# Mixture rows turned by DMA transposes instead of TensorE, two groups ahead

## The reference, cut to what matters

```python
# h: (64, 197, 192); every token is a row of 192 numbers
x2 = layernorm(h).reshape(-1, 192)
weights, indices = gate(x2, gate_weight, gate_bias)   # sigmoid scores, 2 of 4 groups, 2 of 8 experts
h1 = einsum('td,eid->tei', x2, w1)                    # eight experts, each 192 -> 128
h3 = einsum('td,eid->tei', x2, w3)
y  = einsum('tei,edi,te->td', silu(h1) * h3, w2, cw)  # weighted by the gate
z  = silu(x2 @ sw1.T) * (x2 @ sw3.T) @ sw2.T          # a shared expert, added without a weight
out = h + y + z
```

## Time and profile before

| what | value |
|---|---|
| median of three runs | 1811.99 us |
| profiled execution, its own time | 1810.96 us |
| its span | 1809.2 us |
| second stage, from the first load of `hin` | from 1048.72 us to the end |
| PE / DVE / ACT / POOL busy over the span | 94% / 72% / 54% / 19% |

### The profile page before, as it was taken

One profiled execution on the slowest core, in us unless ns is written; L12 is line 12 of the kernel. 1 busy time (PEld: TensorE's weight loads), 2 busy tenths in 40 slices (PEclk: granted clock), 3 DMA queues, 4 the chain that ended last, 5 costly groups with the idle time before them and its releaser, 6 DMA issues. The chain is left out here.

```text
span 1809.2 us, 45442 instructions
## 1 busy us (share of the span) xinstructions
PE 1704.5 (94%) x17682; PEld 1172.8 (65%) x17682; DVE 1297.7 (72%) x3626; ACT 978.8 (54%) x2079; POOL 336.6 (19%) x402
## 2 busy tenths in 40 slices
PE   1899999999999999999999859999999999999998
PEld 1677777777777777777777535555565555555555
DVE  4566666666666666666666448888888888888887
ACT  2466656656655655566666534545545454545453
POOL 1000000000000000000000014343434444343433
PEclk9999999999999999999999969999999999999999
DMA  6232333322223332233330010101010000001000
GB/s 203 62 72 72 73 72 73 72 66 68 69 71 73 72 70 69 72 72 73 72 72 19 15 39 19 36 18 36 19 37 27 28 28 27 28 27 35 17 18 16
DMA packets 40866, 95.26 MB, mean 53 GB/s; under 512 B 4491, under 2 KB 17454, under 8 KB 40526
## 3 DMA queue, kind: packets, MB, share of 16 engines
q1 hardware_dynamic: 31438, 72.89, 12.9%
q0 software_dynamic: 9216, 19.47, 7.0%
HBM read 92.44 MB, written 19.37 MB: 62 GB/s over the span
## 5 line engine op out<-in xcount | busy, mean ns | idle before, releaser
L598 ACT ACTIVATE prob<-ps_sc 99x792 f32<-99x792 f32 x384 | 317.3, 827 | 56.4 <-PE ps_sc L440 56.4
L1259 POOL TENSOR_TENSOR in_lo<-inner,in_hi 128x512 f16<-128x512 f32 (+1 forms) x225 | 257.6, 1145 | 433.6 <-ACT act L1046 433.2
L1192 DVE SCALAR_TENSOR_TENSOR acc<-ps_y,comb,acc 128x192 f32<-128x192 f32 (+1 forms) x700 | 242.0, 408 | 0.3 <-PE ps_y L988 0.3
L1054 ACT ACTIVATE in_hi<-inner 128x512 f16<-128x512 f32 (+1 forms) x225 | 140.3, 623 | 181.3 <-DVE inner L1174 181.3
L1046 ACT ACTIVATE act<-ps_h 128x512 f32<-128x512 f32 (+1 forms) x225 | 131.7, 585 | 189.7 <-PE ps_h L972 189.7
L1174 DVE SCALAR_TENSOR_TENSOR inner<-ps_h,act 128x512 f32<-128x512 f32 (+1 forms) x225 | 153.8, 683 | 103.3 <-ACT act L1046 99.6
L383 PE MATMUL ps_hid<-lin_hi,x_hi 128*99 128x192 f16 x768 | 191.0, 249 | 39.0 <-DVE x_lo L661 34.9
L986 PE MATMUL ps_y<-w_hi,in_hi 128*128 128x192 f16 (+1 forms) x900 | 223.9, 249 | 4.0 <-DVE acc L1192 2.6
L987 PE MATMUL ps_y<-w_lo,in_hi 128*128 128x192 f16 (+1 forms) x900 | 221.4, 246 | 0.0
L988 PE MATMUL ps_y<-w_hi,in_lo 128*128 128x192 f16 (+1 forms) x900 | 221.4, 246 | 0.0
L807 POOL DMA_DIRECT2D x_hi<-xp x64 | 34.0, 532 | 915.4 <-PE ps_hid L385 893.7
(11 more groups left out here) (156 smaller groups left out, 3658.6 us busy)
## 6 DMA issues: line engine op xcount, KB each, us to landing
xin<-xp SPq DMA_DIRECT2D x64, 594.0 KB, 4.4
x_hi<-xp POOLq DMA_DIRECT2D x64, 297.0 KB, 4.0
hidden_dram<-h SPq DMA_DIRECT2D x64, 147.0 KB
hin<-hidden_dram SPq DMA_DIRECT2D x24, 384.0 KB, 3.0
out<-acc SPq DMA_DIRECT2D x24, 384.0 KB, 2.3
w_f<-w SPq DMA_DIRECT2D x1, 2304.0 KB, 9.9
hidden_dram<-h SPq DMA_DIRECT2D x64, 0.8 KB
w_f<-w SPq DMA_DIRECT2D x1, 864.0 KB, 11.9
```

The source lines that it names most:

```text
L598: act.activation(prob[quad][:, places].rearrange("p h m s -> p h (m s)"), ps_sc[0:TR, places, 0:2 * SLOTS], ACT.Exp, scale=D ** -0.5 / (SQ ...
L1192: last = dve.scalar_tensor_tensor(out=acc[p][0:R, t, :], in0=ps_y[half_no][0:R, u * C:(u + 1) * C], scalar=comb[p][0:R, t, e:e + 1], in1=b ...
L1259: pool.tensor_tensor(in_lo[b][:, 0:N], inner[b][:, 0:N], in_hi[b][:, 0:N], ALU.subtract).then_inc(inlo_done, 1)
```

## The change

The normalised rows are no longer turned by TensorE. ScalarE normalises two groups ahead (steps 5 and 6) and writes the fp16 high part `y_hi` from `bnorm` by rows; VectorE writes the low part `y_lo` (steps 6 and 7); SyncE then issues 16-bit DMA transposes of `y_hi` and `y_lo` into `yT_hi` and `yT_lo`, now rings of three. That is four lanes of two transposes, eight for each group, each of 128 rows by 256 columns (columns 192 to 255 repeat 128 to 191). The factor 64 (`SX`) moves from the copies into `rstds`. `y_hi` and `y_lo` have one buffer each, so ScalarE waits with the next group's `y_hi` until the transposes before have landed (`yT_in`). The statistics are at steps 2 and 3, `rstds` moves from behind step 5 to behind step 4, the gate's matmuls from step 4 to step 3, its `Tanh` (`gate_out`) from step 4 to 3, and the parts of `route` from steps 5 to 8 to steps 4, 5, 6 and 8. TensorE's gate waits for all eight transposes. The two banks `ps_x` become one, `ps_gate`.

```diff
@@ -829,9 +829,11 @@
-        bnorm = sb("bnorm", [128, T, 256])
-        yT_hi = [sb(f"yT_hi{p}", [128, 2, GT], F16) for p in range(2)]
-        yT_lo = [sb(f"yT_lo{p}", [128, 2, GT], F16) for p in range(2)]
+        bnorm = sb("bnorm", [128, T, C])
+        y_hi = sb("y_hi", [128, T, 256], F16)
+        y_lo = sb("y_lo", [128, T, 256], F16)
+        yT_hi = [sb(f"yT_hi{p}", [128, 2, GT], F16) for p in range(3)]
+        yT_lo = [sb(f"yT_lo{p}", [128, 2, GT], F16) for p in range(3)]
...
@@ -912,12 +915,29 @@
                 sp.wait_ge(acc_done, g.times(2 * NE, 2 * NE))
                 sp.dma_start(part(tokens_out, g), acc[p][0:rows_of(g)]).then_inc(acc_out[p], 16)
 
+            def transposes(g, half_no):
+                R, p = rows_of(g), g.mod(3)
+                sp.wait_ge(ylo_done, g.times(2, half_no + 1))
+                if half_no == 0 and reached(g.times(NE, -2 * NE)):
+                    sp.wait_ge(inner_done, g.times(NE, -2 * NE))
+                for t in (2 * half_no, 2 * half_no + 1):
+                    s = slice(t * R, (t + 1) * R)
+                    sp.dma_start_transpose(yT_hi[p][:, :, s], y_hi[0:R, t, :]).then_inc(yT_in[p], 16)
+                    sp.dma_start_transpose(yT_lo[p][:, :, s], y_lo[0:R, t, :]).then_inc(yT_in[p], 16)
+
             for g in range(3):
                 load(Index(0, g, 2, GROUPS_B))
+            for g in range(2):
+                transposes(Index(0, g, 2, GROUPS_B), 0)
+                transposes(Index(0, g, 2, GROUPS_B), 1)
 
             def body(g):
+                ahead = g.back(-2)
                 if g.back(-3).active():
                     load(g.back(-3))
+                if ahead.active():
+                    transposes(ahead, 0)
+                    transposes(ahead, 1)
                 store(g)
             run(body)
             sp.wait_ge(acc_out[0], 16 * (FULL // 2 + 1))
...
@@ -925,25 +945,15 @@
 
         @block.tensor
         def _(pe):
-            def transposes(g):
-                R = rows_of(g)
-                pe.wait_ge(bnorm_done, g.times(2, 2))
+            def gate(g):
+                R, p = rows_of(g), g.mod(3)
+                pe.wait_ge(yT_in[p], 32 * T * (g.c // 3 + 1))
 
                 if reached(g.times(1)):
                     pe.wait_ge(tanh_done, g.times(1))
                 for t in range(T):
                     s = slice(t * R, (t + 1) * R)
-                    for k in range(2):
-                        last = pe.transpose(ps_x[k][:, s], bnorm[0:R, t, k * 128:(k + 1) * 128], id32[0:R, 0:R])
-                last.then_inc(yT_done, 1)
-
-            def gate(g):
-                R, p = rows_of(g), g.mod(2)
-                pe.wait_ge(yThi_done, g.times(2, 2))
-                pe.wait_ge(yTlo_done, g.times(2, 2))
-                for t in range(T):
-                    s = slice(t * R, (t + 1) * R)
-                    dst = ps_x[0][0:R, t * E:(t + 1) * E]
+                    dst = ps_gate[0:R, t * E:(t + 1) * E]
                     pe.matmul(dst, yT_hi[p][:, 0, s], gate_hi[:, 0], start=True, stop=False)
                     pe.matmul(dst, yT_hi[p][:, 0, s], gate_lo[:, 0], start=False, stop=False)
                     pe.matmul(dst, yT_lo[p][:, 0, s], gate_hi[:, 0], start=False, stop=False)
...
@@ -1000,9 +1005,7 @@
                         outer_products(g, e - 2)
                     elif g.back(1).active():
                         outer_products(g.back(1), e + NE - 2)
-                    if e == 2 and following.active():
-                        transposes(following)
-                    if e == 4 and following.active():
+                    if e == 3 and following.active():
                         gate(following)
                 if not following.active():
                     outer_products(g, NE - 2)
...
@@ -1014,27 +1017,27 @@
             def normalise(g, half_no):
 
                 R, p = rows_of(g), g.mod(3)
+                ts = slice(2 * half_no, 2 * half_no + 2)
                 act.wait_ge(bneg_done, g.times(1, 1))
+                if reached(g.times(2, half_no - 1)):
+                    act.wait_ge(ylo_done, g.times(2, half_no - 1))
+                for t in (2 * half_no, 2 * half_no + 1):
+                    last = act.activation(bnorm[0:R, t, :], hin[p][0:R, t, :], ACT.Identity,
+                                          scale=brstd[0:R, t:t + 1], bias=bshift[0:R, t:t + 1])
+                last.then_inc(bnorm_done, 1)
+                act.wait_ge(bnorm_done, g.times(2, half_no + 1))
+
                 if half_no == 0 and reached(g.times(1)):
-                    act.wait_ge(yT_done, g.times(1))
-                for t in (2 * half_no, 2 * half_no + 1):
-                    for dst, src in ((slice(0, C), slice(0, C)), (slice(C, 256), slice(128, C))):
-                        last = act.activation(bnorm[0:R, t, dst], hin[p][0:R, t, src], ACT.Identity,
-                                              scale=brstd[0:R, t:t + 1], bias=bshift[0:R, t:t + 1])
-                last.then_inc(bnorm_done, 1)
-
-            def yT_out(g):
-                N, p = T * rows_of(g), g.mod(2)
-                act.wait_ge(yT_done, g.times(1, 1))
-                for k in range(2):
-                    act.activation(yT_hi[p][:, k, 0:N], ps_x[k][:, 0:N], ACT.Copy,
-                                   scale=SX).then_inc(yThi_done, 1)
+                    before = g.back(1)
+                    act.wait_ge(yT_in[before.mod(3)], 32 * T * (before.c // 3 + 1))
+                act.activation(y_hi[0:R, ts, 0:C], bnorm[0:R, ts, :], ACT.Copy)
+                act.activation(y_hi[0:R, ts, C:256], bnorm[0:R, ts, 128:C], ACT.Copy).then_inc(yhi_done, 1)
 
             def gate_out(g):
                 R = rows_of(g)
                 act.wait_ge(gate_done, g.times(1, 1))
 
-                act.activation(half[0:R], ps_x[0][0:R, 0:T * E].rearrange("p (t e) -> p t e", e=E), ACT.Tanh,
+                act.activation(half[0:R], ps_gate[0:R, 0:T * E].rearrange("p (t e) -> p t e", e=E), ACT.Tanh,
                                scale=0.5 / SS).then_inc(tanh_done, 1)
 
             def silu(g, e):
...
@@ -1054,21 +1057,21 @@
                 act.activation(in_hi[b][:, 0:N], inner[b][:, 0:N], ACT.Copy).then_inc(inhi_done, 1)
 
             first = Index(0, 0, 2, GROUPS_B)
+            second = first.back(-1)
             normalise(first, 0)
             normalise(first, 1)
-            yT_out(first)
+            normalise(second, 0)
+            normalise(second, 1)
             gate_out(first)
 
             def body(g):
-                following = g.back(-1)
+                following, ahead = g.back(-1), g.back(-2)
                 for e in range(NE):
                     silu(g, e)
                     inner_first(g, e)
-                    if e in (0, 1) and following.active():
-                        normalise(following, e)
-                    if e == 2 and following.active():
-                        yT_out(following)
-                    if e == 4 and following.active():
+                    if e in (5, 6) and ahead.active():
+                        normalise(ahead, e - 5)
+                    if e == 3 and following.active():
                         gate_out(following)
             run(body)
 
...
@@ -1088,13 +1091,13 @@
                 for t in ts:
                     dve.bn_aggr(bmv[0:R, t, :], bstats[0:R, t, :]).then_inc(bmv_done, 1)
 
-            def yT_out(g):
-                N, p = T * rows_of(g), g.mod(2)
-                for k in range(2):
-                    dve.wait_ge(yThi_done, g.times(2, k + 1))
-                    dve.scalar_tensor_tensor(out=yT_lo[p][:, k, 0:N], in0=ps_x[k][:, 0:N], scalar=SX,
-                                             in1=yT_hi[p][:, k, 0:N], op0=ALU.mult,
-                                             op1=ALU.subtract).then_inc(yTlo_done, 1)
+            def rest_of(g, half_no):
+                R = rows_of(g)
+                ts = slice(2 * half_no, 2 * half_no + 2)
+                dve.wait_ge(yhi_done, g.times(2, half_no + 1))
+                dve.tensor_tensor(y_lo[0:R, ts, 0:C], bnorm[0:R, ts, :], y_hi[0:R, ts, 0:C], ALU.subtract)
+                dve.tensor_tensor(y_lo[0:R, ts, C:256], bnorm[0:R, ts, 128:C], y_hi[0:R, ts, C:256],
+                                  ALU.subtract).then_inc(ylo_done, 1)
 
             ROUTE_STEPS = 19
             ROUTE_PARTS = (0, 3, 7, 11, 13, 15, ROUTE_STEPS)
...
@@ -1207,7 +1210,10 @@
             dve.wait_ge(bneg_done, 1)
             for half_no in range(2):
                 stats_of(second, half_no)
-            yT_out(first)
+            for half_no in range(2):
+                rest_of(first, half_no)
+            for half_no in range(2):
+                rest_of(second, half_no)
             for part_no in range(4):
                 route(first, part_no)
 
...
@@ -1221,12 +1227,14 @@
                         accumulate(g.back(1), e + NE - 2)
                     if e < 2:
                         route(g, e + 4)
```

(33 more changed lines are left out.)

## The result

The changed kernel takes 1879.2 us (median of four runs, 1877.71 to 1879.72) against 1812.47 before: a ratio of 1.037, with a 95% interval of 1.0352 to 1.0388. It is slower by 67 us, where 42 were forecast (1854). That is as forecast in sign and in the wait that starts the loss. The time lies above the forecast's own range (1840 to 1872) and inside the range over all (1836 to 1970), which was stretched upwards for slow transposes.

The account below looks back on a forecast made before the run. TensorE's own instruction list was taken as the bound. Stalls of 23 x 2.6 = 59.8 us less 20.9 saved, +38.9, and +3.5 at the start gave 1854 us; own range 1840 to 1872, over all 1836 to 1970.

Parts of the forecast that it names:

- The bound and the saving: Second stage: TensorE never waits, its list sets the period; dropping 0.87 us of transposes in 24 bodies saves 20.9 us.
- The wait on `rstds` ahead of silu(6): ScalarE, step 5: waits 2.24 us for `rstds`; silu(6) 2.85 us late where 0.9 was free, TensorE stalls 1.9 and 0.15.
- One term of the sum: ScalarE's half in step 5: two activations of 192 columns, mean 531 ns, reach the second's real end after 1.06 us.
- What follows in step 8: TensorE before step 8's outer products: silu(7) late too, 0.43 us more stall, and 0.15 again at the second half.
- Behind it the lists run even again: After steps 7 and 8 ScalarE has two to three free steps; no further stall beyond 2.6 us a body.
- The low part in VectorE's steps 6 and 7: Two operations a half, 0.56 and 0.29 us, 1.4 us for two halves, hidden by VectorE's wait for the late silu.
- DMA transposes: Eight a group on SyncE's queue, taken at 0.6 us each; they cost the loop nothing.
- the point from which they decide: DMA transposes in the loop are free up to 1.6 us each; beyond that the gate in step 3 waits.
- Rival 1: Transposes over 1.6 us each make TensorE's gate wait: 1946 us at 2.1 each, about 2050 at 2.6; chance 23%.
- The start: Second stage's start: eight transposes at 0.6 us and landing before the first gate, +3.5 us, from 0 to +9.
- The 1 us added for the second group: At the stage's start, ScalarE and VectorE prepare the second group before the first gate's routing: about 1 us more.
- Rival 2: Faster: the wait on `bneg_done` and the half behind it fit into the cover, giving 1795 to 1804 us; chance 9%.

Follow-up runs that it names:

- e1_rstds3: The changed kernel with `rstds` moved from behind in_lo(4) to behind in_lo(3), one step earlier: 1798.85 us, 0.9917 of the kernel before.
- e3: The kernel before, with TensorE's transposes, only `rstds` moved behind step 4 and `normalise` two groups ahead in steps 5 and 6: 1894.05 us.
- e4: The kernel before with two extra unused VectorE operations a body, one with two SBUF inputs and one with a single input: 1812.4 us.
- e8: The changed kernel, order untouched, with one input of each 128x256 comparison of `route` moved to PSUM: 1857.65 us.
- e5: e1_rstds3 with every DMA transpose issued twice, the second into scratch that nothing reads, sixteen a group: 2034.18 us.
- e7_first_by_pe: e1_rstds3 with the first group alone transposed by TensorE, the rest by DMA: 1796.68 us, 0.9914 of the kernel before; run again, 1794.94 us.
- e6_later_halves: The changed kernel with `rstds` left behind step 4 and the halves one step later on ScalarE (6, 7) and VectorE (7, 8): 1837.19 us.

## Why the prediction was right, and where its sizes were off

- *The bound and the saving.* Right: TensorE's list sets the period, and 0.87 us went (28.81 in e1_rstds3).
- *The wait on `rstds` ahead of silu(6).* Right in place and size: 2.12 us measured for the 2.24 that I had from the end of in_hi(5); silu(6) 2.7 us late for the 2.85 worked out; 1.86 us more in step 7 against 2.05. Shown by taking it away (e1) and by making it alone (e3). One term of the sum had 0.09 us too much: two activations of 531 ns that follow 0.09 closer end 0.97 behind the start of the first, not 1.06; measured 0.98.
- *What follows in step 8.* 0.36 against 0.58.
- *"Behind it the lists run even again."* This step failed. Steps 0 and 1 lost another 0.38 and 0.97 us, 1.35 a body, 31 us in all. I had priced VectorE's operations by rows of the kernel before, and there, in the steady part, none with two SBUF inputs meets in_lo: GpSimd starts 0.17 us behind a silu, and VectorE is then at its multiply and sums, which read PSUM. A silu that comes late shifts both lists against each other. e4 shows the hold by itself; e8, and the body of 31.17 us, show that without it on the low part steps 0 and 1 have no stall, a price of 1.31 us. One row of the kernel before already had it, outside the steady part that I read, in the last group of 80 rows:

```profile
L1122 DVE TENSOR_TENSOR eq<-eq,bef 80x256 f32<-80x256 f32 x1 | 1.3, 1261 | 0.0
```

- *The low part in VectorE's steps 6 and 7.* The durations interpolated were right (0.56 and 0.29 us; measured 0.55 and 0.28 where nothing holds them), the claim that the wait hides them only without the hold.
- *DMA transposes.* The value taken, 0.6 us, was half of the 1.29 measured; the point from which they decide, 1.6 us, held, so the loop did not notice, and e5 shows the other side of it. The 1309 ns that the Trainium skill gives in "VectorE: DVE Perf Modes", section "The three transpose paths", for 128x128 is about what one of 128x256 takes here (1.29 us of the queue), so the page's figure counted by area would have been twice too high. Rival 1 did not come, by 0.3 us a transpose against the point worked out; in the trace the room is larger, since the last one lands 5 us before the gate. The time given there for 2.1 us each took 0.45 us beyond that point, where 2.1 - 1.6 is 0.5; it should have been 1955.
- *The start.* +6.9 against +3.5. The transposes were ready when forecast (9.96 us behind the first load for 9.9), but from the first issue to the gate it is 11.5 us for the 7.1 of the forecast: at 1.29 us each, 4.4 more. The 1 us added for the second group did not come: from the first inner product to that of step 5 it is 18.34 us, and 19.02 before, of which 0.87 are transposes.
- *Rival 2*, faster if the wait fits the cover, is what e1_rstds3 is: 1799 to the 1795 to 1804 worked out. The condition named for it, silu(6) able to start in time, is what that run brought about.
- *Luck.* The measured time is outside the forecast's own range. It is inside the range over all because the upper end was held open for slow transposes, and they were not what filled it.

The sum of the misses, in us: 31.0 for the collisions, 3.4 for the start and 1.3 from the first stage, less 9.4 for steps 7 and 8 (0.41 a body), are 26.3; forecast and median are 25.2 apart.

## What to carry to other kernels

When work is moved ahead in an engine's list, check what it waits for and what is queued behind it: one wait of 2.1 us placed ahead of the instruction that all others follow cost 80 us over 23 bodies, with the collisions that it brought, and one step more between producer and consumer made it free. A delay of one engine also changes which instructions of two others coincide; durations from a trace hold only for the coincidences of that trace. A long latency that a ring hides in the loop is paid in full once, at the start, where the first group may be done the old way.

## What the runs showed of the hardware that I had not expected

- A DMA transpose of 128x256 16-bit elements within SBUF takes 1.29 us of the issuing queue, and eight or sixteen follow one another at that pitch, with a single longer one now and then (1.71 us in e5_sixteen, 2.11 in e7_first_by_pe); it lands 2.3 to 2.4 us after its issue.
- A VectorE tensor_tensor with both inputs in SBUF that starts beside a GpSimd tensor_tensor is held until 0.14 to 0.28 us after its end (0.96 in place of 0.42 us, up to 1.37); the multiply, with one input in PSUM, keeps its 0.69 us beside an in_lo, and a reduce with a single input its 0.41. Which of the two is held differs between bodies of one program whose starts differ by 0.06 us (in_lo 1.67 us and low part 0.28, or 1.40 and 1.24, in the changed kernel), and in e6_later_halves with starts that agree within 0.01.
- TensorE's granted clock stayed at 1.00 through the changed kernel's idle times of up to 1.72 us. It fell to 0.50 once behind one of 2.08 us (e8_ties_in_psum), and in every body of e5_sixteen, where it stood at 0.50 for 4.0 to 5.3 us of work behind an idle time of about 7 in the three bodies read. An idle time of 2.42 us in e7_first_by_pe left it at 1.00.
